# Second stage of a two-stage transformer block: two of three norms scaled by ScalarE, and row maxima turned by three engines and a DRAM buffer instead of TensorE

## The reference

```
x = x + (n + P)                 n = layernorm(x); attention A: 16 heads of 64, softmax, exact GELU, Wpost
x = x + ffn(layernorm(x))       ternary W1 (256 to 1024), relu, ternary W2, biases        "ffn0"
x = x + attn_b(layernorm(x))    16 heads of 16, biases, RoPE on q and k, softmax, wo      "attn"
x = x + ffn(layernorm(x))       the same ffn                                              "ffn1"

layernorm(x) = (x - mean) / sqrt(var + 1e-5)
attn_b: logits = q k^T / 4; softmax over keys; y = softmax @ v; y @ wo + wo_b
```

## Time and profile before

| | us |
|---|---|
| median of 3 runs (lowest, highest) | 3813.62 (3811.97, 3814.59) |
| profiled execution, its own time | 3815.57 |
| its span | 3813.7 |
| PE busy | 3650.5 (96%) |
| DVE, ACT, POOL busy | 2720.9, 2330.4, 1917.1 |

### The profile page before, as it was taken

The page is one execution under the profiler, slowest core; times in us unless marked ns, Lnnn a source line. Parts: engine busy times, 40 slices in busy tenths (PEclk is TensorE's granted clock), DMA queues, the critical chain, the costliest instruction groups (busy, mean ns, idle before and its releaser), DMA issues.

```text
span 3813.7 us, 64079 instructions
## 1 busy us (share of the span) xinstructions
PE 3650.5 (96%) x23938; PEld 2451.6 (64%) x23938; DVE 2720.9 (71%) x4342; ACT 2330.4 (61%) x4501; POOL 1917.1 (50%) x1210
## 2 busy tenths in 40 slices
PE   8999999999999999999999878999999999999987
PEld 5777777777777777777777654555555555555534
DVE  6766666667676666666667667888888888888762
ACT  5665666566566656656656435666666666666654
POOL 4555555545555555555555433555555555555412
PEclk9999999999999999999999988999999999999988
DMA  2000000000000000000000012222222222222220
GB/s 78 7 12 1 12 12 12 1 12 12 1 12 12 7 7 12 12 1 12 12 1 15 25 48 56 52 58 61 59 57 61 58 57 57 57 57 57 51 45 17
DMA packets 86965, 114.16 MB, mean 30 GB/s; under 512 B 6660, under 2 KB 60420, under 8 KB 86660
## 3 DMA queue, kind: packets, MB, share of 16 engines
q1 hardware_dynamic: 86660, 110.07, 11.5%
HBM read 33.43 MB, written 25.17 MB: 15 GB/s over the span
## 4 chain that ended last, share of the span: by engine, by line
PE 84%; DVE 9%; ACT 3%; issue 2%; POOL 2%; DMA 0%; DVEq 0%; POOLq 0%; ACTq 0%
PE ps_o L642 12%; PE ps_s L611 10%; PE ps_t L624 8%; PE ps_t L218 7%; PE ps_o L718 6%; PE ps_t L753 5%; PE ps_s L691 5%; PE ps_m L624 4%; PE ps_t L225 4%; PE ps_t L744 4%; PE ps_m L218 4%; PE ps_t L677 3%; DVE max_b L1114 3%; PE ps_s L705 3%; PE ps_m L744 2%
## 5 line engine op out<-in xcount | busy, mean ns | idle before, releaser
L511 POOL TENSOR_TENSOR e_a<-e_a,recip 128x1024 f32<-128x1024 f32 x512 | 969.4, 1894 | 955.7 <-DVE recip L983 955.6
L796 ACT ACTIVATE e_a<-ps_s,neg_max 128x512 f32<-128x512 f32 x1024 | 694.3, 685 | 548.5 <-DVE neg_max L976 548.2
L1114 DVE TENSOR_REDUCE max_b<-ps_s 128x2 f32<-128x1024 f32 x512 | 623.6, 1219 | 177.7 <-PE ps_s L691 176.0
L838 ACT ACTIVATE et<-ps_s 128x1024 f32<-128x1024 f32 x512 | 523.7, 1023 | 357.1 <-PE ps_s L705 356.8
L976 DVE TENSOR_REDUCE neg_max<-ps_s 128x2 f32<-128x1024 f32 x512 | 622.7, 1216 | 68.7 <-PE ps_s L611 68.7
L642 PE MATMUL ps_o<-et_a,v_a 128*64 128x256 f32 x4096 | 500.2, 386 | 9.6 <-DVE heads_a L1019 5.2
L611 PE MATMUL ps_s<-raw_a 64*128 64x512 f32 x3072 | 426.0, 409 | 8.8 <-ACT e_a L796 8.7
L543 POOL TENSOR_TENSOR h_lo<-h,h_hi 128x512 fp32r<-128x512 f32 x248 | 320.5, 1305 | 183.1 <-ACT h_hi L880 183.1
L642 PEld LDWEIGHTS ps_o<-et_a,v_a 128*64 128x64 f32 x4096 | 279.6, 137 | 192.8 <-issue 79.2
L990 DVE COPY et_a<-ps_t 128x512 f32<-128x512 f32 x366 | 250.9, 687 | 207.0 <-PE ps_t L624 202.8
L624 PE MATMUL ps_t<-ident,e_a 128*128 128x128 f32 x2660 | 395.0, 281 | 2.1 <-DVE xl L1164 2.0
(11 more groups left out here) (196 smaller groups left out, 7315.7 us busy)
## 6 DMA issues: line engine op xcount, KB each, us to landing
q_stack<-roped_q SPq DMA_DIRECT2D x256, 96.0 KB
k_stack<-roped_k SPq DMA_DIRECT2D x256, 96.0 KB
x_a<-X SPq DMA_DIRECT2D x16, 512.0 KB, 3.9
X<-x_a SPq DMA_DIRECT2D x16, 512.0 KB, 2.9
x_ahead<-X SPq DMA_DIRECT2D x16, 512.0 KB, 3.8
X<-x_ahead SPq DMA_DIRECT2D x16, 512.0 KB, 4.9
x_before<-X SPq DMA_DIRECT2D x16, 512.0 KB, 3.8
OUT<-x_before SPq DMA_DIRECT2D x16, 512.0 KB, 5.1
```

Source lines behind the costliest of these rows:

```text
L511: nc.gpsimd.tensor_tensor(e_a[:, u % 5, :, :], e_a[:, u % 5, :, :], factor, ALU.mult).then_inc(e_normed, 1)
L796: ins = nc.scalar.activation(e_a[:, u % 5, h, :], ps_s[:, 2 * (u % 2) + h, :], ACT.Exp, bias=neg_max[:, u % 5, h:h + 1], accum_out=sums[:, ...
L838: nc.scalar.activation(et[:, v % 5, :, :], ps_s[:, 2:4, :], ACT.Exp)\
L1114: nc.vector.reduce_max(max_b[:, u // 4 % 2, :, u % 4], ps_s[:, score_bank(u):score_bank(u) + 2, :], AX.X, negate=True).then_inc(max_done, 1)
```

## The change

Norms of ffn0 and attn are scaled by ACT: xn = rstd * x + shift, with shift = -mean * rstd. DVE makes `minus_mean` in `aggregate`, POOL makes `shift` behind the power. ffn1's norm stays with DVE. Statistics of both norms, their scaling, the attn bias, and the save and load of x move to other steps. The PE transposition of the maxima is gone, with its fills of the three banks: ACT makes the high part of 128 x 8 maxima (`max_high`), POOL the low part (`max_low`), DVE transposes 32 x 32 blocks (`turn_max`), SP writes the turned rows to a DRAM buffer `M1` (`save_max`) and reads them back into `q_stack` (`max_rows`).

```diff
+        shift = at("shift", 1.4375, [P, TB])
+        minus_mean = at("minus_mean", 1.46875, [P, TB])
-        m_rows = at("m_rows", 32, [P, 2, 2, P], F32R)
+        m_parts = at("m_parts", 32, [P, 2, 32], F32R)
+        m_turned = at("m_turned", 33, [P, 2, 32])
...
-        NORM = {"ffn0": (-108, -106, -105, -103, -98), "attn": (-67, -64, -63, -60, -58), "ffn1": (103, 108, 109, 113, 115)}
-        BIAS = {"ffn0": -88, "attn": -57, "ffn1": 124}
+        NORM = {"ffn0": (-104, -103, -101, -95, -91), "attn": (-67, -64, -63, -51, -49), "ffn1": (103, 108, 109, 113, 115)}
+        BIAS = {"ffn0": -88, "attn": -47, "ffn1": 124}
...
-            plan += [(8 * p + 9.25, "max", "attn", p, s) for p in range(PAIRS)]
...SP
+                def save_max(s, pair):
+                    sp.wait_ge(max_turned, PAIRS * s + pair + 1)
+                    if s or pair >= 2:
+                        sp.wait_ge(max_in[(pair - 2) % PAIRS], 2 * 16 * (s + (pair >= 2)))
+                    sp.dma_start(M1[pair % 2, :, :].rearrange("r (q c) -> q r c", q=4), m_turned[:, pair % 2, :]).then_inc(max_out, 16)
+
                 def max_rows(s, pair):
                     if s == 0 and pair == 0:
                         sp.wait_ge(key_ones_in, 2 * 16)
-                    wait_emptied(sp, fill_of["max", "attn", pair, s])
-                    for part in range(2):
-                        sp.dma_start(q_stack[48 + part:P:64, pair, :].bitcast(F32), m_rows[0:8, pair % 2, part, :].bitcast(F32))\
-                            .then_inc(max_in[pair], 16)
+                    sp.wait_ge(max_out, 16 * (PAIRS * s + pair + 1))
+                    for h in range(2):
+                        rows = M1[pair % 2, 0:16, :].rearrange("(p h t) c -> h p (t c)", p=2, h=2)[h, :, :]
+                        sp.dma_start(q_stack[64 * h + 48:64 * h + 50, pair, :].bitcast(F32), rows).then_inc(max_in[pair], 16)
-                            if r == -115:
+                            if r == -108:
                                 load_ahead(s)
-                            if r == -54:
+                            if r == -46:
                                 save_ahead(s)
                             if r in STACK:
                                 stack(s, STACK.index(r))
+                            if r >= 10 and (r - 10) % 8 == 0 and (r - 10) // 8 < PAIRS:
+                                save_max(s, (r - 10) // 8)
                             if r >= 12 and (r - 12) % 8 == 0 and (r - 12) // 8 < PAIRS:
                                 max_rows(s, (r - 12) // 8)
...POOL
+                    if part != "ffn1":
+                        pool.wait_ge(rstd_ready, nth_norm[part, s] + 1)
+                        nc.gpsimd.tensor_tensor(shift[:, :], minus_mean[:, :], rstd[:, :], ALU.mult).then_inc(shift_ready, 1)
...
+                def max_low(n):
+                    pool.wait_ge(m_high, n + 1)
+                    nc.gpsimd.tensor_tensor(m_parts[:, n % 2, 8:16], max_b[:, n % 2, :, :].rearrange("p h t -> p (h t)"),
+                                            m_parts[:, n % 2, 0:8], ALU.subtract).then_inc(m_low, 1)
...
                     for step in (2 * (slot - SHIFT), 2 * (slot - SHIFT) + 1):
+                        if step % 8 == 0 and 8 <= step < 2 * UNITS_ALL + 8:
+                            max_low((step - 8) // 8)
...PE: the kind "max" (L761) is gone
...ACT
+                def normalise(part, s, first):
+                    act.wait_ge(shift_ready, nth_shift[part, s] + 1)
+                    if part == "ffn0" and s == 0:
+                        act.wait_ge(a_x_out, 16 * (BATCH - 1))
+                    for t in (first, first + 1):
+                        nc.scalar.activation(xn[:, t, :], x_of[part][:, t, :], ACT.Identity, scale=rstd[:, t:t + 1],
+                                             bias=shift[:, t:t + 1]).then_inc(xn_ready, 1)
...
+                def max_high(n):
+                    act.wait_ge(max_done, 4 * n + 4)
+                    if n >= 2:
+                        act.wait_ge(max_turned, n - 1)
+                    nc.scalar.activation(m_parts[:, n % 2, 0:8], max_b[:, n % 2, :, :].rearrange("p h t -> p (h t)"), ACT.Copy)\
+                        .then_inc(m_high, 1)
...
+                        if step % 8 == 0 and 8 <= step < 2 * UNITS_ALL + 8:
+                            max_high((step - 8) // 8)
                         if step % 2 == 0 and 0 <= step // 2 - L < UNITS_ALL:
                             exps(step // 2 - L)
+                        for piece, part, s in norm_steps.get(step, []):
+                            if piece > 2 and part != "ffn1":
+                                normalise(part, s, 2 * (piece - 3))
...DVE
+                    nc.vector.tensor_scalar(minus_mean[:, :], mean_var[:, :, 0], -1.0, None, ALU.mult)
                     nc.vector.tensor_scalar(rstd[:, :], mean_var[:, :, 1], EPS, None, ALU.add).then_inc(var_ready, 1)
...
                 def unit_max(u):
                     dve.wait_ge(qk_done, u + 1)
+                    if u % 4 == 0 and u >= 8:
+                        dve.wait_ge(m_low, u // 4 - 1)
...
+                def turn_max(s, pair):
+                    n = PAIRS * s + pair
+                    dve.wait_ge(m_low, n + 1)
+                    if n == 0:
+                        dve.wait_ge(m_set, 1)
+                    if n >= 2:
+                        dve.wait_ge(max_out, 16 * (n - 1))
+                    nc.vector.transpose(m_turned[:, pair % 2, :], m_parts[:, pair % 2, :].bitcast(F32)).then_inc(max_turned, 1)
...
+                        if step % 8 == 2 and 10 <= step < 2 * UNITS_ALL + 10:
+                            turn_max((step - 10) // SLOT, (step - 10) % SLOT // 8)
                         if step % 2 == 0 and 0 <= step // 2 < UNITS_ALL:
                             unit_max(step // 2)
...
-                            else:
+                            elif part == "ffn1":
                                 normalise(part, s, 2 * (piece - 3))
...
+    m1 = nc.dram_tensor("M1", (2, 32, 128), mybir.dt.float32, kind="Internal").ap()
```

More of the change, by code:

```diff
@@ L3, with hybrid_block_kernel @@
 from contextlib import ExitStack
-def hybrid_block_kernel(nc, X, WQ, WK, WV, WPOST, WB, BQK, BV, WO, BO, W1T, B1, W2T, B2, COS, SIN, X1, OUT):
+def hybrid_block_kernel(nc, X, WQ, WK, WV, WPOST, WB, BQK, BV, WO, BO, W1T, B1, W2T, B2, COS, SIN, X1, M1, OUT):
     F32, F32R = mybir.dt.float32, mybir.dt.float32r
@@ L166, in hybrid_block_kernel @@
         a_xn_ready = sem("a_xn_ready")
+        shift_ready = sem("shift_ready")
         xn_ready = sem("xn_ready")
@@ L190, in hybrid_block_kernel @@
         copied = sem("copied")
+        m_set = sem("m_set")
         m_high = sem("m_high")
+        m_low = sem("m_low")
+        max_turned = sem("max_turned")
+        max_out = sem("max_out")
         max_in = [sem(f"max_in{i}") for i in range(PAIRS)]
@@ L346, in hybrid_block_kernel @@
         nth_norm = {(part, s): n for n, (_, part, s) in enumerate(norms)}
+        nth_shift = {(part, s): n for n, (_, part, s) in enumerate(norm for norm in norms if norm[1] != "ffn1")}
         norm_steps = {}
@@ L758, in product @@
                         last = token_major(half, xh, xl, wb_hi, wb_lo, i, 2 * D, D)
[L759 to L762, removed]
                     if kind not in ("wo", "down", "v") or i % 2 == 1:
@@ L1063, in set_value_ones @@
                     nc.vector.memset(v_b[:, :, :, :, HB:32], 1.0).then_inc(ones_set, 1)
+                    nc.vector.memset(m_parts[:, :, 16:32].bitcast(F32), 0.0).then_inc(m_set, 1)
                 def scale_biases():
@@ L1088, in normalise @@
                     dve.wait_ge(rstd_ready, nth_norm[part, s] + 1)
-                    if part == "ffn0" and s == 0:
-                        dve.wait_ge(a_x_out, 16 * (BATCH - 1))
                     for t in (first, first + 1):
@@ L1164, in empty_low @@
                         emptied(nc.vector.tensor_tensor(xl[:, i, :], bank(fill), xh[:, i, :], ALU.subtract), fill)
[L1165 to L1168, removed]
                 for slot in range(FIRST_A, LAST + SHIFT):
@@ L1273 @@
     x1 = nc.dram_tensor("X1", arrays["X"].shape, mybir.dt.float32, kind="Internal").ap()
+    m1 = nc.dram_tensor("M1", (2, 32, 128), mybir.dt.float32, kind="Internal").ap()
     out = nc.dram_tensor("OUT", arrays["X"].shape, mybir.dt.float32, kind="ExternalOutput").ap()
-    hybrid_block_kernel(nc, *args, x1, out)
+    hybrid_block_kernel(nc, *args, x1, m1, out)
     r = run_bass_kernel_spmd(nc, [arrays], core_ids=[0])
```

## The result

| | before | after |
|---|---|---|
| median, us | 3814.11 (4 runs) | 3864.06 (4 runs) |
| profiled execution: its span | 3813.7 | 3862.3 |
| PE, DVE, ACT, POOL busy | 3650.5, 2720.9, 2330.4, 1917.1 | 3671.5, 2578.5, 2388.0, 1939.3 |

The ratio after to before is 1.0127, 95% interval 1.0115 to 1.0139: 1.3% slower. The direction was forecast, the size was not: 3828 us with a range up to 3854, against 3864.

A forecast was written before the change was run, and what follows sets the result against it. PE was taken as the bound (84% of the chain), with waits at few places. 3815.57 + 14 x (1.3 - 0.33) - 5.5 + 6.5 = 3830.2 us profiled, 3828 as a median, range 3792 to 3854.

The forecast's parts named there:

- POOL's added work ends the rotations 2.1 us later: POOL, slots 11 to 18: two max_low add 0.55 and 0.23 us, ffn0's moved power and shift 1.30.
- ACT's scaling, 0.40 us an instruction: ffn0's scaling on ACT: 0.40 us for 128 x 256 (bounds 0.25 and 0.63), 0.8 for two.
- PE's wait before slot 19 is 3.2 us: Late rotations delay the exps of slot 18, so PE waits 3.2 us before slot 19's L705 instead of 1.25.
- The clock falls in 5 of 14 batches, 1.3 us each, +6.5 us in all (0 to 18): After slot 19's longer wait PE's granted clock falls more often than in two of thirteen batches: +6.5 us.
- Slots 12 to 21, +1.3 us without the clock: These slots get 1.3 us longer a batch (-0.9 to +2.3), with slot 21's DVE wait of 0.86 us gone.
- Saved transposes 0.33 us a batch, of n = 5, 6 and 7: Eight removed PE transposes of maxima at 0.11 us each; only these three pay, the others stand before waits.
- DVE waiting for `max_low` in front of `unit_max`: Sign of a wrong forecast: turn_max, ahead of unit_max on DVE, waits for POOL; it was taken as hidden.
- The start, -5.5 us: Lead-in and first two batches, where DVE is the bound, gain 5.5 us in all (0 to -9).
- The DRAM way is late: Rival, 12%: for n = 1, max_rows takes 8.7 of 8.8 us available; 3 us lateness gives 3856 us.
- the prediction's 4 us: Estimate from 2.0 us fixed per DMA: the detour through DRAM is 4 us longer than a direct copy, inside 8.8.
- the prediction's own price: Each removed PE transpose of the maxima priced at 0.11 us, eight a batch 0.88 us.

The follow-up runs named there:

- highs_before: The kernel before, with ACT's two last rotated halves behind the exps of slots 18 and 19 and DVE's low parts two steps later: 3793.95 us.
- highs_after: The changed kernel with the ACT and DVE order of highs_before and the second pair of ffn0's xn one step earlier: 3827.13 us.
- cheap_power: The changed kernel with a product in place of the power of ffn0's norm on POOL: 3830.55 us.
- low_after: The changed kernel with POOL's max_low put behind hidden_low of the same step: 3832.91 us.
- filled: The changed kernel with 12 extra matmuls on PE ahead of the turned scores of slot 19: 3842.39 us.
- max_only: The changed kernel with the norm part undone, so only the new way of the maxima remains: 3834.12 us.
- norm_only: The kernel before with only the norm part of the change, the maxima still going through PE: 3821.52 us.

## Why the prediction was wrong in size

- *POOL's added work ends the rotations 2.1 us later.* Right in its mechanism, 1.7 us instead of 2.1. `max_low` takes 0.203 us (0.23 said), `shift` 0.268 (0.23), each as mean; the start of the rotations was forecast at 1.66 us behind the score of slot 12 and is at 1.62, the end at 19.8 and is at 19.4, with 17.7 before:

```profile
L868 ACT ACTIVATE xn<-x_ahead,shift,rstd 128x256 f32<-128x256 f32 x124 | 66.9, 590 | 8.4 <-POOL shift L550 8.4
L566 POOL TENSOR_TENSOR m_parts<-max_b,m_parts 128x8 fp32r<-128x8 f32 x119 | 24.1, 203 | 531.2 <-ACT m_parts L902 531.2
L550 POOL TENSOR_TENSOR shift<-minus_mean,rstd 128x4 f32<-128x4 f32 x31 | 8.3, 268 | 2.4
```

- *ACT's scaling, 0.40 us an instruction.* It is 0.590 in the trace and two of them take 1.08. Too low by 0.3 us a pair; it stood where ACT had room.
- *PE's wait before slot 19 is 3.2 us.* 2.73. The mechanism holds: highs_before and highs_after take it away by the order on ACT and DVE, cheap_power by POOL's chain.
- *The clock falls in 5 of 14 batches, 1.3 us each, +6.5 us in all (0 to 18).* This is the step that failed most. It fell in all eleven batches from 2 to 12 and costs 1.8 us each, 25 us in 14 batches. I scaled two cases behind a wait of 1.25 us; behind a wait twice as long it fell in eleven of eleven batches here and in eight of eleven in low_after. Both the count and the price were too low, the upper bound of 18 too.
- *Slot 28* had no term. It is 1.11 us a batch, about 16 us in 14. I worked out which waits `max_low` adds for n = 2 and 3 and that for n = 4, but not for n = 6, and did not ask what stands behind it on POOL. low_after shows the cause.
- *Slots 12 to 21, +1.3 us without the clock.* filled has 8.01 us in slots 19 and 20 and 2.73 in 21, against 7.34 and 2.72: +0.7. Slots 14, 16 and 17 add 0.3, so about 1.0.
- *Saved transposes 0.33 us a batch, of n = 5, 6 and 7.* Those of n = 5 and 7 show, 0.22 us; that of n = 6 shows only in low_after (slot 28 at 2.80 against 2.91). Slots 4 and 12 (n = 0 and 2) are shorter too, 0.46 us with the first two, but slot 5 grew by 0.22, and slot 12 stands ahead of the wait of slot 19, as forecast.
- *DVE waiting for `max_low` in front of `unit_max`,* named as a sign of being wrong. It occurs: `turn_max` waits 0.96 us in slot 5, 11.6 us in twelve batches. PE is not held by it: the max behind it ends at 2747.31, and the next score starts at 2749.20.

```profile
2745.99 0.21 DVE L1163 STREAM_TRANSPOSE m_turned<-m_parts 128x32 f32<-128x32 f32 x1 [0.96 <-POOL m_parts L566]
```

- *The start, -5.5 us.* The first score came 3.9 us earlier, but unit 64 only 0.3. The first two batches lost 5.6 us in slot 19, 1.4 in slot 28 and 3.4 in slots 3, 5 and 7 of the second batch, whose mean granted clock is 0.89 (0.92 before), and won a part of it back elsewhere.
- *The DRAM way is late.* PE waited for no DMA of `q_stack`. SP waited 193.4 us in 98 times for M1's DMA, so 2.0 us each; a `save_max` issued at 2783.46 let `max_rows` go at 2785.46:

```profile
SPq L479 <- DMA M<-m_turned: 193.4, 98, 4.1
```

  By this, the figure of about 2 us that the Trainium skill gives in "DMA: Bandwidth & Descriptors", section "Anatomy of one DMA — SWDGE (gpsimd) path", agrees with this trace, though it was measured on another issuing path. The detour puts one DMA more in front of the one that was there, so the prediction's 4 us are for both together, not for the detour alone.

Sum of a batch: 1.8 and 0.1 (clock, in slots 19 and 20 and in 21) + 1.1 (slot 28) + 0.7 (slots 19 and 20 without it) + 0.5 (slots 5, 14 to 17) - 0.5 (transposes) = 3.7, of 3.81 measured.

## What to carry to other kernels

Before a small instruction is put on an in-order engine, list for every place of it what waits behind it and whether its input is ready there; here 0.2 us of `max_low` cost 1.1 us where it waited for another engine. A wait on TensorE has a second price once it lowers the granted clock, and this price comes in jumps: in max_only four waits of 1.07, 0.46, 0.91 and 0.66 us left the clock at 1.00 in all eleven batches, three of 0.68, 1.02 and 0.66 lowered it in three of eleven in cheap_power, one of 1.39 us, with 0.49 us ahead of it, in eight in norm_only, and one of 2.73 us in all eleven and, in low_after, in eight. And look first at the order on the engine that PE waits for: moving two ACT instructions behind the exps, and DVE's low parts with them, gained 0.6%, where all eight transposes of a batch were worth 0.88 us, 0.3%, by the prediction's own price.

## What I had not expected of the hardware

A DVE TENSOR_SCALAR of 128 x 4 values took 1.02 us where POOL ran a two-input operation of 1.28 us beside it; the next one of the same size took 0.16. It is so in every batch from 2 to 12, and without a POOL operation beside it L1123 takes 0.17:

```profile
2773.78 1.02 DVE L1123 TENSOR_SCALAR minus_mean<-mean_var 128x4 f32<-128x4 f32 x1
2774.71 0.16 DVE L1124 TENSOR_SCALAR rstd<-mean_var 128x4 f32<-128x4 f32 x1
```

Filling a wait of 2.7 us with twelve useless matmuls made the kernel 22 us faster (3842.39 against 3864.06), and what changed is the granted clock: 1.00 in all eleven batches.
